# A graph layer's sort, layer norm and mixing: statistics moved to ScalarE, the message projection into the sort, the residual onto TensorE

## What is computed

```
xn  = layernorm(x)
gnn = segment_sum(weight * (xn @ gnn_W)[dst], src) + gnn_b
q, k = elu(xn @ Wq.T) + 1, elu(xn @ Wk.T) + 1 ;  v = xn @ Wv.T        (8 heads of 32)
mix = (q @ (k.T @ v)) / (q @ sum(k)) @ Wproj.T + bproj
x1  = x + gnn + mix
out = x1 + moe(layernorm(x1))      (8 experts, 2 per row, 256 -> 512 -> 256)
```

## Time and profile before

| | us |
|---|---|
| median of 3 runs (lowest, highest) | 4866.37 (4864.51, 4872.25) |
| the profiled execution, its own time | 4830.11 |
| its span, first to last instruction | 4827.9 |
| TensorE busy, share of the span | 3178.2, 66% |
| VectorE | 2635.4, 55% |
| GpSimd | 2654.3, 55% |
| ScalarE | 470.9, 10% |
| mean granted TensorE clock | 0.798 of 2.4 GHz |

### The profile page before, as it was taken

The page is one execution under the profiler, slowest core; times in us unless marked ns, Lnnn a source line. Parts: engine busy times, 40 slices in busy tenths (PEclk is TensorE's granted clock), DMA queues, the critical chain, the costliest instruction groups (busy, mean ns, idle before and its releaser), DMA issues.

```text
span 4827.9 us, 59941 instructions
## 1 busy us (share of the span) xinstructions
PE 3178.2 (66%) x16092; PEld 2426.5 (50%) x16093; DVE 2635.4 (55%) x5891; ACT 470.9 (10%) x971; POOL 2654.3 (55%) x2745
## 2 busy tenths in 40 slices
PE   5644443286666666665666666666566688999993
PEld 5643442274454444444445544454455455666662
DVE  8886972544444444445766776676565211233325
ACT  0100000140000000000000000000012111112110
POOL 0087875016666666666666666666616777135521
PEclk9955555697777777777888888878755899999997
DMA  9222222553333333333333333333542322223316
GB/s 324 80 88 62 93 71 86 182 209 101 100 101 100 101 101 100 100 99 101 101 98 100 100 101 100 98 102 100 84 97 83 109 85 87 66 91 107 110 64 222
DMA packets 330492, 519.67 MB, mean 108 GB/s; under 512 B 70411, under 2 KB 233955, under 8 KB 330403
## 3 DMA queue, kind: packets, MB, share of 16 engines
q0 software_dynamic: 113584, 277.66, 20.2%
q1 hardware_dynamic: 168129, 193.09, 12.5%
q10 hardware_dynamic: 48690, 47.73, 2.9%
HBM read 378.80 MB, written 136.92 MB: 107 GB/s over the span
## 4 chain that ended last, share of the span: by engine, by line
PE 29%; DVE 22%; issue 18%; another core or an unknown queue 15%; DVEq 6%; POOL 5%; DMA 4%; SPq 1%; ACT 0%; POOLq 0%; ACTq 0%
DVE acc L1856 8%; PE bank L1472 7%; PE bank L1454 6%; DVE select L1847 5%; PE bank L1272 5%; POOL lists L683 4%; DVEq L56 3%; PE bank L1464 2%; DMA lists<-placed,dest_i 2%; PE bank L1247 2%; DVE relu_kq L1943 2%; DVEq L1856 1%; DVE onehot L1576 1%; PE bank L1373 1%
## 5 line engine op out<-in xcount | busy, mean ns | idle before, releaser
L718 POOL DMA_INDIRECT message<-h_table,gather_stage x1660 | 1590.8, 958 | 1124.5 <-issue 496.6
L1272 PE MATMUL bank<-message,select 128*128 128x256 f32 x3320 | 1006.6, 459 | 372.9 <-DVE select L1847 227.7
L1856 DVE TENSOR_TENSOR acc<-acc,bank 128x256 f32 x1660 | 697.7, 420 | 855.9 <-remote 583.9
L1272 PEld LDWEIGHTS bank<-message,select 128*128 128x128 f32 x3320 | 747.9, 233 | 620.6 <-DVE select L1847 291.1
L683 POOL DMA_INDIRECT lists<-placed,dest_i x300 | 451.4, 1505 | 341.2 <-DVE dest_i L1694 238.1
L1847 DVE TENSOR_SCALAR select<-iota_n,gather_stage 128x128 f32<-128x128 f32 x1660 | 463.8, 359 | 12.2 <-DMA gather_stage<-records 8.8
L1472 PE MATMUL bank<-w,hid_t 128*128 x1696 | 403.2, 391 | 28.3 <-ACT hid_t L1045 16.5
L1278 PE MATMUL bank<-w_cat,xt_in 128*128 128x256 f32 x784 | 256.4, 438 | 224.7 <-issue 222.7
L1454 PE MATMUL bank<-w,fx_t 128*128 x848 | 386.5, 599 | 0.1
L1472 PEld LDWEIGHTS bank<-w,hid_t 128*128 128x128 f32 x1696 | 323.5, 197 | 76.2 <-issue 34.4
L2166 DVE TENSOR_TENSOR fy<-bank,b 128x256 f32<-128x256 f32 x212 | 89.7, 425 | 477.6 <-PE bank L1472 294.6
(11 more groups left out here) (289 smaller groups left out, 3702.3 us busy)
## 6 DMA issues: line engine op xcount, KB each, us to landing
rows<-block_dram SPq DMA_DIRECT2D x75, 514.5 KB
fx<-x_sorted SPq DMA_DIRECT2D x212, 128.0 KB
message<-h_table,gather_stage POOLq DMA_INDIRECT x1660
xt_in<-xt_dram SPq DMA_DIRECT2D x98, 256.0 KB
x_sorted<-zeros_list ACTq DMA_DIRECT2D x1, 15360.0 KB, 117.7
w<-y_token SPq DMA_DIRECT2D x28, 512.0 KB, 5.3
lists<-zeros_list SPq DMA_DIRECT2D x8, 1664.0 KB, 27.4
read_back<-lists SPq DMA_DIRECT2D x13, 1024.0 KB, 5.8
```

The source lines that it names most:

```text
L718: pool.indirect_dma_start(out=message[:, slot % SETS, j, :], out_offset=None, in_=h_table, in_offset=Offset(ap=gather_stage[:, slot, j, 0: ...
L1272: last = nc.tensor.matmul(ps, select[:, slot % 2, j, :], message[:, slot % SETS, j, :], start=True, stop=True)
L1856: added = V.tensor_tensor(to, to, ps, ALU.add)
```

## The change

- **Statistics in the counting.** SyncE loads x in 13 groups of 8 blocks into `x_buf` (three groups at a time) right behind the edges, ahead of the blanking of the lists. ScalarE takes each block's sum (Identity with an accumulator) and sum of squared differences (Square with a bias), then one square root; VectorE makes row_scale and row_shift from them before the tables. The blanking of x_sorted moves from ScalarE's queue to SyncE's: the first half behind the lists, the second half and number_sorted behind the first three row loads and the first four pairs of x.
- **Projection in the second pass.** x is loaded a second time, pair by pair, two pairs a batch. ScalarE normalises (scale and bias), TensorE transposes into bank 5 or 6, ScalarE copies, TensorE multiplies with `gnn_w` into bank 0 or 1, ScalarE copies, SyncE stores both; four buffers each.
- **Read-back.** The bias and mixing weights are loaded around the first pieces of the lists. GpSimd fills `acc` with the bias in 7 copies of 14 blocks. Stage 4 is gone.
- **Residual.** `acc` no longer starts from x. Each mixing unit loads its pair of x (`bring_x`, 256 KB), and TensorE adds it as identity times x ahead of the product with mix_w, in the same bank.
- Smaller: ScalarE masks the last pair's v, semaphores are merged.

```diff
@@ SyncE @@
+            sp.dma_start(gnn_w[:, :, :], gnn_W.rearrange("(k p) n -> p k n", p=P)).then_inc(s_first_w, 16)
...
+            for j in range(3):
+                load_group(j)
+            sp.wait_ge(s_block, 1)
+            sp.dma_start(block_dram.rearrange("(s p j) -> p s j", p=P, j=P),
+                         block_a[:, :, :].rearrange("p (s h) j -> p s (h j)", h=2)).then_inc(s_block_dram, 16)
+            sp.wait_ge(s_block_dram, 16)
+            for j in range(3, XGROUPS):
+                sp.wait_ge(s_x_read, j - 2)
+                load_group(j)
...
             for h in range(G8):
...
+            blank_tiles(0)
...
+            def store_pair(g):
+                sp.wait_ge(s_xt, g + 1)
+                sp.dma_start(xt_dram[g], x_buf[:, 6 + g % 4, :]).then_inc(s_xt_out[g % 4], 16)
+                sp.wait_ge(s_h_read, g + 1)
+                sp.dma_start(h_pairs[g], pair_of(10 + g % 4)).then_inc(s_h_out[g % 4], 16)
...
             for c in range(STEP):
                 bring_rows(c)
+            sp.wait_ge(s_x_read, XGROUPS)
+            for g in range(4):
+                load_pair(g)
+            blank_tiles(1)
...
             for c in range(STEP, K):
                 sp.wait_ge(s_hot_t, c - STEP + 1)
                 bring_rows(c)
+                m = c // STEP - 1
+                if c % STEP == STEP - 1 and m:
+                    for g in range(2 * m - 2, 2 * m):
+                        store_pair(g)
+                    for g in range(2 * m + 2, min(2 * m + 4, PAIRS)):
+                        load_pair(g)
...
+            sp.dma_start(bias_in[:, 0, :], gnn_b.partition_broadcast(P)).then_inc(s_first_w, 16)
+            sp.dma_start(bias_in[:, 1, :], mix_bproj.partition_broadcast(P)).then_inc(s_first_w, 16)
             for seg in range(RSEG):
+                if seg == 2:
+                    sp.dma_start(w_nat[:, 0:2, :], mix_Wq.rearrange("(a p) c -> p a c", p=P)).then_inc(s_wload, 16)
...
@@ GpSimd @@
+            pool.wait_ge(s_first_w, 48)
+            steps.done(pool.tensor_tensor(bias_row[:, :], bias_in[:, 0, :], bias_in[:, 1, :], ALU.add))
+            steps.settle()
+            for a in range(0, NB, 14):
+                acc_made = pool.tensor_copy(acc[:, a:a + 14, :], bias_row[:, :].unsqueeze(1).to_broadcast([P, 14, C]))
+            acc_made.then_inc(s_late, 1)
@@ ScalarE @@
+            def row_stats(j):
...
+                for i in range(n):
+                    b = first + i
+                    steps.done(act.activation(rows_of[:, i, :], rows_of[:, i, :], ACT.Identity, accum_out=row_sum[:, b:b + 1]))
+                steps.settle()
+                steps.done(act.activation(row_neg[:, first:first + n], row_sum[:, first:first + n], ACT.Copy, scale=-1.0 / C))
+                steps.settle()
+                for i in range(n):
+                    b = first + i
+                    squared = act.activation(rows_of[:, i, :], rows_of[:, i, :], ACT.Square, bias=row_neg[:, b:b + 1],
+                                             accum_out=row_sq[:, b:b + 1])
+                squared.then_inc(s_x_read, 1)
...
+            for m in range(M):
+                g = 2 * m
+                normalise(g)
+                copy_placed(STEP * m)
+                copy_xt(g)
+                if g + 1 < PAIRS:
+                    normalise(g + 1)
+                copy_placed(STEP * m + 1)
+                copy_h(g)
+                if g + 1 < PAIRS:
+                    copy_xt(g + 1)
+                copy_placed(STEP * m + 2)
+                if g + 1 < PAIRS:
+                    copy_h(g + 1)
@@ TensorE @@
             for m in range(M):
                 if m + 1 < M:
                     look(m + 1)
-                for c in range(STEP):
-                    place(m * STEP + c)
+                g = 2 * m
+                place(m * STEP)
+                transpose_rows(g)
+                place(m * STEP + 1)
+                project(g)
+                if g + 1 < PAIRS:
+                    transpose_rows(g + 1)
+                place(m * STEP + 2)
+                if g + 1 < PAIRS:
+                    project(g + 1)
...
                         pe.wait_ge(s_qn, g + 1)
                         if not first:
                             pe.wait_ge(s_mix_added, g)
+                        pe.wait_ge(s_x_in[half], i * 16 + (16 - 16 * (MIX_TURN // 2 + 1)) + (32 if isinstance(g, int) and g == PAIRS - 1 else 0))
                         for u in range(2):
+                            nc.tensor.matmul(bank[6][:, u * C:(u + 1) * C], ident[:, :], x_in[:, half, u, :], start=True, stop=False)
                             for h in range(KC):
                                 last = nc.tensor.matmul(bank[6][:, u * C:(u + 1) * C],
                                                         act_kq[:, h * C + u * P:h * C + (u + 1) * P], mix_w[:, h, :],
-                                                        start=(h == 0), stop=(h == KC - 1))
+                                                        start=False, stop=(h == KC - 1))
@@ VectorE @@
-            dve.wait_ge(s_late, 2)
-            dve.wait_ge(s_x, 16 * len(XCUT))
-            all_row_stats()
...
-            invert_std(1, 0, NB, newton[:, :])
...
-            add_bias(PAIRS - 1)
+            dve.wait_ge(s_late, 3)
```

More of the change, by code:

```diff
@@ L478, in _ @@
                 bring_rows(c)
+                m = c // STEP - 1
[4 more added lines that the diff above has]
+                        load_pair(g)
+            for g in range(2 * M - 4, PAIRS):
+                store_pair(g)
             sp.wait_ge(s_blank, 48)
@@ L528, in _, with bring_x @@
                 stage_list(half, half)
-            for slot in range(2):
-                sp.wait_ge(s_xt_out[slot], 16 * ((PAIRS + 1 - slot) // 2))
             bring_xt(PAIRS - 1, 0)
             bring_xt(0, 1)
+            def bring_x(i, half):
+                pair = i * 2 + (half - MIX_TURN - 1)
+                if isinstance(pair, int) and pair == PAIRS - 1:
+                    sp.wait_ge(s_mix, pair - 1)
+                    load_last_pair(sp, x_in[:, half, :, :], s_x_in[half])
+                else:
+                    if not isinstance(pair, int):
+                        sp.wait_ge(s_mix, pair - 1)
+                    sp.dma_start(x_in[:, half, :, :], x_pairs[ds(pair, 1), :, :, :].rearrange("a p u c -> p (a u) c")).then_inc(s_x_in[half], 16)
             def stage_turn(i, half, free=None, need=None, pair=None):
@@ L552, in _ @@
             B1 = MIX_TURN // 2 + 1
-            stage_turn(B1, 0, s_v_psum, PAIRS, 0)
-            stage_turn(B1, 1, s_v_psum, PAIRS, 1)
+            for half in range(2):
+                stage_turn(B1, half, s_v_psum, PAIRS, half)
+                bring_x(B1, half)
             with sp.Fori(B1 + 1, MIX_TURN) as i:
@@ L916, in _, with normalise, copy_xt, copy_h @@
                     act.activation(rank_g[:, a:a + n], ps[:, 0:n], ACT.Copy, scale=0.5).then_inc(s_turned_out, 1)
-            for c in range(K):
+            act.wait_ge(s_row_scale, 1)
+            def normalise(g):
+                act.wait_ge(s_x_pair[g % 4], 16 * (g // 4 + 1) if g < PAIRS - 1 else 16 * (g // 4 + 3))
+                if g >= 2:
+                    act.wait_ge(s_xt_psum, g - 1)
+                for u in range(2):
+                    b = 2 * g + u
+                    scaled = act.activation(x_buf[:, 4 + g % 2, u * C:(u + 1) * C], x_buf[:, g % 4, u * C:(u + 1) * C], ACT.Identity,
+                                            bias=row_shift[:, b:b + 1], scale=row_scale[:, b:b + 1])
+                scaled.then_inc(s_xn, 1)
+            def copy_xt(g):
+                act.wait_ge(s_xt_psum, g + 1)
+                if g >= 4:
+                    act.wait_ge(s_proj, g - 3)
+                    act.wait_ge(s_xt_out[g % 4], 16 * (g // 4))
+                act.activation(x_buf[:, 6 + g % 4, :], bank[5 + g % 2][:, :], ACT.Copy).then_inc(s_xt, 1)
+            def copy_h(g):
+                act.wait_ge(s_proj, g + 1)
+                if g >= 4:
+                    act.wait_ge(s_h_out[g % 4], 16 * (g // 4))
+                act.activation(x_buf[:, 10 + g % 4, :], bank[g % 2][:, :], ACT.Copy).then_inc(s_h_read, 1)
+            def copy_placed(c):
                 act.wait_ge(s_placed, c + 1)
```

301 lines of the change are left out of this document (138 added, 163 removed).

## The result

The changed kernel takes 4737.62 us (median of 3 runs, 4729.98 to 4741.0), a ratio of 0.9723 [0.9702, 0.9744] to the kernel before: 128.7 us less. The forecast of 4770 was 32 us too high, on the right side and inside its range. The profiled execution took 4729.98 us (span 4728.3, granted clock 0.820).

A forecast was written before the change was run, and what follows sets the result against it. GpSimd's scatters bound the second pass, then a serial chain of statistics and projection delays the gathers. -187 + 20 + 20 + 6 + 45 = -96 us, applied to the median 4866.4: 4770 us, range 4695 to 4860.

The forecast's parts named there:

- Removed stage: Between read-back and gathers: without the serial chain of statistics and projection the first gather could start at 870, saving 187 us.
- cover of the statistics: In the counting: ScalarE's 85 us of statistics, about 20 to 105, delay nothing; 0 taken, bounds 0 to 10 us.
- fill of acc: Around read-back: GpSimd's bias fill takes 22 to 51 us from about 808, done by 860, before the first gather.
- Second blanking: Before the second pass: the moved blanking delays the fourth row load and first scatter; 20 us taken, bounds 0 and 25.
- Coupling in the pass: In the second pass: coupled queues let VectorE run less far ahead of GpSimd; 20 us taken, bounds 0 and 100.
- Mixing units: Identity products after the wait for act_kq lengthen the 49 units by 0 to 93 us in all; half, 45, taken.
- Rival 1: All additions hide: stalls absorb the identity products, the pass gains no waits; -161 us, 4705 us; chance 0.27.
- Rival 2: Mixing units pay in full, 93 us, and the pass 40; sum -28 us, 4838 us; chance 0.16.
- Rival 3: Second pass becomes TensorE's, over 22 us a batch; at 30 us +200, 4930 us or so; chance 0.07.
- clock above 0.57: In the second pass: TensorE's granted clock would rise above the 0.57 it had before.
- few waits for placed: In the second pass: GpSimd's waits for placed buffers would stay well under 60 us.
- context units as before: In the context gathers: 23.6 us from one such wait of GpSimd to the next, unchanged.

The follow-up runs named there:

- the early blankings: Changed kernel with the lists' blanking between the loads of x and both x_sorted halves and number_sorted before the row loads: 4650.65 us, ratio 0.9653.
- the doubled products: Changed kernel with each projection in the second pass computed twice (392 more products): 4698.79 us, ratio 0.9745.
- the projection behind the pass: Changed kernel with normalising, transposing and projecting of the 49 pairs after the second pass, statistics still in the counting: 4807.81 us, ratio 0.997.
- the products left out: Changed kernel without the two identity products of each mixing unit, the transfer of x_in kept: 4678.5 us, ratio 0.9706.
- the tripled ones: Changed kernel with each identity product of the mixing units issued three times: 4698.5 us, ratio 0.973.

## Why the prediction was right, and where it was off

The account by stages, from the spans of the repeat of the changed kernel (4691.5) and the first trace of before (4827.9), both with the faster gathers:

| part | predicted | measured | how |
|---|---|---|---|
| stage 4 gone, read-back | -187 + 6 = -181 | -184.9 | last scatter to first gather, 72.0 against 256.9 |
| first scatter | +20 | +31.4 | 278.3 against 246.9 |
| pass | +20 | +9.7 | 563.2 against 553.5 |
| context part | 0 | -1.2 | 1216.8 against 1218.0 |
| mixing part | +45 | +10.1 | 1156.6 against 1146.5 |
| gathers after it, end | 0 | -1.5 | 97.5 + 1307.1 against 99.9 + 1306.2 |
| sum | -96 | -136.4 | |

With the pass of before at its worked-out 544 and that of the change at 4688.9 - (4693.1 - 563.2) = 559 us, the pass costs 15 and the sum is -131, the measured -132.

- **Removed stage, cover of the statistics, fill of acc: right.** ScalarE's statistics end at 111 (forecast 105), and nothing waits for them; the lists and blankings behind them land before 203. The fill ends at 872, 38 us ahead of the first gather. That this work cost nothing rests on the earlier trace rows: ScalarE was empty, and so were the rings from 120 to 203.
- **Second blanking: right mechanism, size 11 us short.** The term that was mis-sized is "11776 KB at 343 GB/s are 35 us". The half that stands behind the first row loads has 15360 KB. Put into the prediction's own sum, it takes 46 us, the rings are free at 257 (it landed at 257.4) and the fourth row load lands near 261, where VectorE did start, at 261.41. The 44.15 us of number_sorted's issue are no further cost of those 60 KB: in the kernel before and in the early blankings, too, this issue stands for 48.28 and 45.77 us behind x_sorted and ends 4 to 6 us before its own landing. That the whole +31 came from the transfers put behind the first rows is shown by the early blankings (first scatter 247.4); they moved the half and number_sorted together, so the split between the two is by size. The Trainium skill, DMA: Bandwidth & Descriptors, Issuing engines are not separate DMA queues, has transfers interleave whoever issues them. That speaks of different issuers; here the blanking and the row load stood in one queue, and no run issued this blanking behind 203 from another engine, so the rule was not put to the test.
- **Coupling in the pass: size about right, by another mechanism, so by luck.** I took 20 and it is 15 by the medians (9.7 and 40.5 against the two traces of before). The prediction had GpSimd wait longer for placed buffers. Those waits fell instead, from 23.5 to 8.6 us, and the cost came as longer scatters (mean 1556 ns against 1505 and 1428), which the prediction doesn't have. The statement that a trace gives the length of this pass was the weak one: two executions of the kernel before differ by 31 us in it.
- **Mixing units: wrong size.** "I take half: 45 us" is the term that carries nearly all of the error. It measured 10 us at most (three kernels with the same mixing code on another chip, the early blankings, the doubled products and the projection behind the pass, have mixing parts of 1149.0 to 1149.5, which makes it 2 to 3), and 156 us more of the same work add 3 to 10. The evidence for absorption was in the earlier trace rows: GpSimd waits as long in a context unit, with other work on the chain, as in a mixing unit. I gave it 0.27 of the chance and gave the eight records' 3.78 us more weight. Rival 1 was right in this half and wrong in the other (the pass did not come for nothing, 910 and not 896), though the granted clock rose to 0.72 as it said. Rival 2's 93 us are out by the products left out and by the tripled ones. Which wait does set the 23.9 us of a unit is open.
- **A sum of Rival 3.** At 30 us a batch its +200 gives -187 + 20 + 6 + 45 + 200 = +84, some 4950 us and not 4930.
- **Signs named:** clock above 0.57 (0.72), few waits for placed (8.6), context units as before (on like chips) came true; "mixing units longer by about 1 us" did not, it is 10.1 / 48 = 0.2 us.

The 36 us between -96 and -132 are thus -35 of the mixing term, -5 of the pass, -4 of the stage and -3 of the rest, against +11 of the blanking.

## What to carry to other kernels

A serial stage is worth moving when two engines and the rings are idle elsewhere, and its price is then in what it is put in front of: list every transfer that then stands ahead of a needed load and read its size from the DMA issues of the trace, since here the wrong half of one blanking was priced and that was the whole 11 us. Work behind the last wait of a chain is only on the path if that chain sets the period; when two kinds of unit with different chains have the same period and the same stall, that is a sign that it doesn't, and tripling the work tests it. And before a stage's length from one trace goes into a sum, compare what is left of that trace with the median.

## What the runs showed of the hardware

The scatters of the pass fall into classes, and the long ones have one pattern. From the changed kernel's timeline:

```profile
500.54 4.15 POOL L737 DMA_INDIRECT lists<-placed,dest_i  x1 [0.30 <-issue]
500.83 1.55 DVE L1829 TENSOR_TENSOR hot_q<-iota_q,q_pair 128x2688 bf16<-128x2688 bf16 x1
502.30 1.55 DVE L1834 TENSOR_TENSOR hot_w<-hot_r,record 128x1344 f32<-128x1344 bf16 x1
```

This scatter starts before hot_q and ends 0.84 us after the end of hot_w; alone it takes 0.97. So do all 46 of the 300 scatters over 4 us in this trace (0.83 to 0.85 us after that end), all 31 in the first trace of before and all 17 in the second. No scatter that meets neither of the two takes over 2 us. Of those that meet the pair later, 2, 31 and 46 take 2 to 3 us. The three passes' scatter times, 466.9, 451.4 and 428.3 us, follow the number of full catches, so the length of the pass hangs in part on the phase between VectorE's pairs and GpSimd's scatters: 23 of the 31 us between the two executions of the kernel before are scatter time. The other traces fit. With the projection in the pass once, all ten have 45 or 46 full catches, with the doubled products 40, with the projection behind the pass 25. So what the projection costs in the pass goes with this count. This is read from traces; no run here moved the phase alone. The Trainium skill, SBUF — State Buffer, SBUF: two separate sides, says that while VectorE holds the port pair that it shares with GpSimd, GpSimd can't write its descriptors and such a transfer only seems to be blocked; these rows agree in that the scatter ends behind VectorE's operations, though they show neither ports nor descriptors.

Also not expected: sum and squares of a 128x256 block take 400 and 492 ns with the read of the accumulator (186 ns) beginning inside that time, while the scale with bias and factor from SBUF takes 595.
